# A GNN stack on one Trainium2 core: the minimum of the shared slots moved from VectorE to ScalarE in layer 0

## The reference

```
h    = max(layernorm(x), 0)
h_jk = relu(h_j @ W1a + (h_j - h_k) @ W1b + b1)      # for each edge j-k, 192 wide
hm_j = sum over k of mask[j,k] * h_jk
x    = x + hm @ W2 + degree * b2
```

## Time and profile before

| what | value |
|---|---|
| median of 3 runs | 1604.89 us (1604.22 to 1605.42) |
| the profiled execution | 1604.63 us |
| its span | 1602.8 us |
| TensorE busy | 1440.3 us (90%) |
| VectorE busy | 1273.2 us (79%) |
| ScalarE busy | 939.7 us (59%) |
| GpSimd busy | 493.8 us (31%) |
| mean granted TensorE clock | 0.971 |

### The profile page before, as it was taken

One profiled execution on the slowest core, in us unless ns is written; L12 is line 12 of the kernel. 1 busy time (PEld: TensorE's weight loads), 2 busy tenths in 40 slices (PEclk: granted clock), 3 DMA queues, 4 the chain that ended last, 5 costly groups with the idle time before them and its releaser, 6 DMA issues. The chain is left out here.

```text
span 1602.8 us, 42482 instructions
## 1 busy us (share of the span) xinstructions
PE 1440.3 (90%) x11815; PEld 1117.8 (70%) x11816; DVE 1273.2 (79%) x3215; ACT 939.7 (59%) x2169; POOL 493.8 (31%) x610
## 2 busy tenths in 40 slices
PE   0799999999999999999999999999799997973298
PEld 0577777777777777777777777777688887930298
DVE  6699999998999999999999999988344445878755
ACT  0756665666656566665666556653355554826675
POOL 1233333333333333333333333333111111047400
PEclk9999999999999999999999999999799999987599
DMA  6000000000000000000000000000000000000022
GB/s 139 14 8 9 14 7 7 7 7 13 7 7 7 7 13 7 7 7 7 13 7 7 7 7 7 6 1 1 1 0 0 0 0 1 0 0 1 3 49 53
DMA packets 40749, 18.09 MB, mean 11 GB/s; under 512 B 19396, under 2 KB 40710, under 8 KB 40710
## 3 DMA queue, kind: packets, MB, share of 16 engines
q1 hardware_dynamic: 40178, 17.39, 4.4%
q10 hardware_dynamic: 532, 0.21, 0.1%
HBM read 13.40 MB, written 4.19 MB: 11 GB/s over the span
## 5 line engine op out<-in xcount | busy, mean ns | idle before, releaser
L785 DVE SCALAR_TENSOR_TENSOR acc<-slot_banks,acc 128x768 f32<-128x768 f32 x512 | 488.1, 953 | 44.8 <-PE slot_banks L551 34.5
L849 POOL TENSOR_TENSOR acc<-acc 128x384 f32<-128x384 f32 x128 | 128.0, 1000 | 679.2 <-DVE onediff L779 675.4
L551 PE MATMUL slot_banks<-ac_hi,work 128*128 128x192 f16 x1408 | 263.9, 246 | 0.0
L551 PE MATMUL slot_banks<-ac_lo,work 128*128 128x192 f16 x1408 | 263.8, 246 | 0.0
L697 ACT ACTIVATE hmTa<-bank,unscale 128x128 f32<-128x128 f32 x128 | 47.0, 367 | 360.9 <-PE bank L527 360.9
L551 PE MATMUL slot_banks<-ac_hi,onediff 128*128 128x192 f16 x1024 | 186.0, 247 | 18.8 <-DVE acc L785 12.7
L551 PE MATMUL slot_banks<-ac_lo,onediff 128*128 128x192 f16 x1024 | 184.8, 246 | 0.0
L544 PE MATMUL slot_banks<-ac_hi,ident 128*128 128x384 f16 x512 | 168.0, 328 | 10.1 <-issue 9.5
L544 PE MATMUL slot_banks<-ac_lo,ident 128*128 128x384 f16 x512 | 167.0, 327 | 0.0
L551 PEld LDWEIGHTS slot_banks<-ac_hi,work 128*128 (+1 forms) x1408 | 137.9, 98 | 16.7 <-issue 0.2
L551 PEld LDWEIGHTS slot_banks<-ac_lo,work 128*128 (+1 forms) x1408 | 137.9, 98 | 16.7 <-issue 0.2
(11 more groups left out here) (251 smaller groups left out, 3283.9 us busy)
## 6 DMA issues: line engine op xcount, KB each, us to landing
adj_in<-in_adj_dram SPq DMA_DIRECT2D x32, 256.0 KB, 2.8
out_dram<-acc SPq DMA_DIRECT2D x32, 128.0 KB, 2.0
l1w<-in_L_gnn_W_dram SPq DMA_DIRECT2D x2, 64.0 KB
l1b<-in_L_gnn_b_dram SPq DMA_DIRECT2D x2, 64.0 KB
x_all<-in_x_dram SPq DMA_DIRECT2D x4, 0.2 KB, 12.0
nm_in<-in_nodemask_dram ACTq DMA_DIRECT2D x1, 64.0 KB
w1a<-in_L_gnn_W_dram ACTq DMA_DIRECT2D x1, 48.0 KB
w1b<-in_L_gnn_W_dram ACTq DMA_DIRECT2D x1, 48.0 KB
```

Of the source, the lines that this page charges most:

```text
L551: last = nc.tensor.matmul(unit(pair, t, 1), hot(t), part[:, q, H:2 * H].unsqueeze(1), start=False, stop=(e == 1 and (t % SB == SB - 1 or t ...
L785: nc.vector.scalar_tensor_tensor(out=sums, in0=unit((q + k) % 2, 0, SU), scalar=0.0, in1=sums, op0=ALU.min, op1=ALU.add).then_inc(s_free[k ...
L849: nc.gpsimd.tensor_tensor(acc[:, q, 0:2 * H], acc[:, q, 0:2 * H], acc[:, q, 2 * H:4 * H], ALU.add)
```

## The change

ScalarE takes the minimum of the shared slots, as Relu of the negative: `act_shared`. Relu(-v) is -min(v, 0), so the host matrix is copied with the scale -1, and the product of the two has the same value as before. `act_shared` for graph b - 1 stands at the head of ScalarE's step b, where VectorE had taken the minimum at the end of its step b - 1. The three slot rank copies leave `act_host_ranks` and become `act_host_slots`; they run in the following step 0, behind the copies of the product. `pool_sum` knew from VectorE's count of `s_free2` that VectorE's sums of the graph were made; for the last graph it now waits for `s_free[1]` too.

```
--- before.py
+++ after.py
@@ -417,7 +417,7 @@
         s_done = [sem(f"own_half{k}_gathered") for k in range(2)]
         s_free = [sem(f"own_half{k}_summed") for k in range(2)]
         s_done2 = sem("shared_slots_gathered")
-        s_free2 = sem("shared_slots_cut")
+        s_free2 = sem("shared_slots_summed")
         s_half = sem("neighbour_sums_paired")
         s_hm = sem("neighbour_sum_ready")
         s_T = sem("sum_transposed")
@@ -661,7 +661,10 @@
         def act_host_ranks(act, g, p):
             act.wait_ge(s_hr, g + 1)
             nc.scalar.activation(ranks2, pA3[:, :], ACT.Copy)
-            nc.scalar.activation(hostT[:, p, :], pH[:, :], ACT.Copy).then_inc(s_hostT, 1)
+            nc.scalar.activation(hostT[:, p, :], pH[:, :], ACT.Copy, scale=-1.0).then_inc(s_hostT, 1)
+
+        def act_host_slots(act, g, p):
+
             act.wait_ge(s_hostT, g + 1)
             for t in range(SS):
                 last = nc.scalar.activation(rs2[:, p, :, t, :], ranks2.rearrange("p (q j) -> p q j", q=GS),
@@ -691,6 +694,14 @@
             nc.scalar.activation(acc[:, q, :].rearrange("p (t h) -> p t h", t=SU),
                                  ac32[:, q % 2, 0:H].unsqueeze(1).broadcast_to([N, SU, H]), ACT.Relu,
                                  scale=neg_pad[:, p, q:q + 1]).then_inc(s_acc0, 1)
+
+        def act_shared(act, b, q):
+
+            if not (known(b) and b < 2):
+                act.wait_ge(s_hm, b - 1)
+            act.wait_ge(s_done2, b + 1)
+            nc.scalar.activation(acc2[:, q % 2, :].rearrange("p (t h) -> p t h", t=SS), unit(q % 2, 0, SS),
+                                 ACT.Relu, scale=-1.0).then_inc(s_free2, 1)
 
         def act_sum(act, b, p, q):
             act.wait_ge(s_T, b + 1)
@@ -818,11 +829,6 @@
                 dve.wait_ge(s_n, g1 + 1)
                 dve.reg_load(count_reg, chunks[0:1, ds(b + 1, 1)])
             late()
-            if not (known(b) and b < 2):
-                dve.wait_ge(s_hm, b - 1)
-            dve.wait_ge(s_done2, b + 1)
-            nc.vector.tensor_scalar(acc2[:, q % 2, :].rearrange("p (t h) -> p t h", t=SS), unit(q % 2, 0, SS),
-                                    0.0, None, ALU.min).then_inc(s_free2, 1)
 
         def dve_update(dve, b):
             xb = x[:, ds(b * F, F)]
@@ -846,6 +852,9 @@
             if not (known(b) and b == B - 1):
                 pool.reg_add(first, total, 1)
                 pool.wait_ge(s_D, first)
+            else:
+                pool.reg_add(first, total, B)
+                pool.wait_ge(s_free[1], first)
             nc.gpsimd.tensor_tensor(acc[:, q, 0:2 * H], acc[:, q, 0:2 * H], acc[:, q, 2 * H:4 * H], ALU.add)
             shared = acc2[:, q % 2, :]
             nc.gpsimd.tensor_tensor(shared[:, 0:H], shared[:, 0:H], shared[:, H:2 * H], ALU.add).then_inc(s_half, 1)
@@ -932,8 +941,11 @@
                 act_pads(act, 0, 0, 0, 0)
                 act_rank_nodes(act, 0)
                 act_host_ranks(act, 0, 0)
+                act_host_slots(act, 0, 0)
 
                 def step(b, g, u, q, nxt, p, use):
+                    if not (known(b) and b == 0):
+                        act_shared(act, b - 1, (q + 3) % GS)
                     if nxt is not None:
                         if q == 1:
                             act_rank(act, nxt, p)
@@ -943,6 +955,8 @@
                             act_rank_nodes(act, nxt)
                     if not (known(b) and b + 2 >= B):
                         act_ac(act, b + 2, (q + 2) % GS)
+                    if q == 0 and not (known(g) and g == 0):
+                        act_host_slots(act, g, u)
                     if not (known(b) and b + 1 >= B):
                         act_pads(act, b + 1, *group_of(b, g, u, q, -1))
                     if nxt is not None:
@@ -958,6 +972,7 @@
                         act_host_ranks(act, nxt, p)
 
                 all_iterations(act, step)
+                act_shared(act, B - 1, 3)
                 act_sum(act, B - 1, 1, 3)
 
             @block.vector
```

More of the change, by code:

```diff
@@ L820, in dve_slots @@
             late()
[L821 to L825, removed]
         def dve_update(dve, b):
```

## The result

The changed kernel takes 1609.62 us (median of 20 runs), the kernel before 1604.75 us (20 runs): ratio 1.0030, 95% interval 1.0023 to 1.0037. It is slower, as forecast, but by 4.9 us and not by 17.4; 1609.6 lies under the range. The profiled execution of the changed kernel has a span of 1608.5 us, 5.7 us over the one before.

A forecast was written before the change was run, and what follows sets the result against it. TensorE was 97% busy, with steps 2 and 3 starting on ScalarE's copy of the sum. A 1.28 us slip less 0.72 us gives 0.56 us a group; 31 groups add 17.4 us to 1604.6: 1622.0 us, range 1611 to 1633.

The forecast's parts named there:

- the idle time at its head: ScalarE's step 1: the minimum waits for the shared slots' last gather, rank copies queued behind it; 1.10 us of waiting.
- the price of the minimum: ScalarE's new instruction: 0.64 us long, delaying the next by 0.54 us, with bounds of 0.41 and 0.86 us.
- the slip of L698: ScalarE's second copy of the transposed sum in step 1 ends 1.28 us later, after 0.36 us are absorbed.
- the fixed 1.31 us: TensorE, steps 2 and 3: the graph's first half starts this long behind the end of ScalarE's copy of the sum.
- the 0.72 us that come back: TensorE's step 2: all that VectorE costs in a group, 0.72 us, goes by TensorE's own lateness.
- the + 0.56 us a group: Net loss per group of four graphs: 1.28 us of slip less 0.72 us, in 31 groups.
- steps 3, 0 and 1 keep their lengths: After step 2's transposes come 0.56 us later, everything following shifts equally and the other steps stay as long.
- priced at nothing: Edits given no cost: the minimum in steps 2, 3 and 0, the moved slot copies, the sign.
- (a): Rival: VectorE's relief in step 2 arrives without ScalarE's delay; 0.65 us a group, 20 us faster, 1584.5 us; 6%.
- (c): Rival: the minimum costs as much as the pads, 0.86 us to the next; 27 us lost, 1632 us; 12%.
- (d): Rival: minimum at its 0.41 us lower bound, 1618 us; with less than the whole 1.31 us paid, 1611; no separate chance.
- if one of the steps 2, 3 and 0 grew by itself: Sign in the changed profile that would show the forecast wrong; these steps were expected to have room for the edits.

The follow-up runs named there:

- run 9: The changed kernel with TensorE's load of the chunk count moved ahead of the product in every step: 1603.31 us, ratio 0.9987 to the kernel before.
- run 2: The changed kernel with only the step-0 graph's minimum on ScalarE, VectorE keeping the other three: 1619.08 us, ratio 1.0087 to the kernel before.
- run 3: The changed kernel with VectorE keeping the step-2 graph's minimum, ahead of step 3's difference: 1617.10 us, ratio 1.0075 to the kernel before.
- run 8: The changed kernel with a spare 256-element GpSimd addition ahead of the low part in step 3: 1617.60 us, ratio 1.0070 to the kernel before.
- run 4: The changed kernel with only the step-2 graph's minimum on ScalarE, VectorE keeping the others: 1601.18 us, ratio 0.9972 to the kernel before.
- run 11: The kernel before with only the three slot rank copies moved from the end of step 3 to step 0: 1604.78 us, ratio 0.9998.
- Run 1: The changed kernel with VectorE keeping the step-0 graph's minimum, so none heads ScalarE's step 1: 1591.81 us, ratio 0.9917 to the kernel before.
- run 6: The changed kernel with the minimum in step 1 behind the first three of eight rank copies: 1587.06 us, ratio 0.9890 to the kernel before.
- run 5: The changed kernel with ScalarE's copies of the sum moved ahead of `h` in step 1: 1603.97 us, ratio 0.9991 to the kernel before.

## Why the prediction was wrong

**Right, and shown.** The order of ScalarE's queue and the idle time at its head (1.26 us); the price of the minimum (0.66 us for 0.64, 0.55 to the next for 0.54); the slip of L698 (1.30 for 1.28); its way through the fixed 1.31 us, which run 9 shows to be the load of the chunk count (0.86 us without it). Right too were the 0.72 us that come back, by TensorE's lateness and not by VectorE's relief (run 2), and so the + 0.56 us a group (0.57).

**The step that failed** is "The transposes of step 2 ... come 0.56 us later, and steps 3, 0 and 1 keep their lengths". They don't. I had weighed VectorE's relief in step 2 alone and found it worth nothing there. The minimum is also gone in front of step 3's difference, and this was priced at nothing without asking what the earlier difference sets off. GpSimd waits for it to sum up the graph. Before, then in the change:

```profile
653.86 1.00 POOL L849 TENSOR_TENSOR acc<-acc 128x384 f32<-128x384 f32 x1 [4.52 <-DVE onediff L779]
```

```profile
659.50 0.99 POOL L858 TENSOR_TENSOR acc<-acc 128x384 f32<-128x384 f32 x1 [3.98 <-DVE onediff L790]
```

It starts 0.80 us behind step 3's first half (659.50 against 658.70) where it was 1.57 us (653.86 against 652.29). So its low part is over when VectorE makes the host rows, and these take 0.73 us for 1.23. The shared one-hot, again before and in the change:

```profile
658.73 0.31 DVE L773 TENSOR_SCALAR work<-work,slot_key 128x384 f16<-128x384 f16 x1
```

```profile
664.64 0.31 DVE L784 TENSOR_SCALAR work<-work,slot_key 128x384 f16<-128x384 f16 x1
```

It is ready 6.25 us behind step 3's first half, for 6.75, so 0.5 us earlier, and TensorE, which waits for it before it can pass the loop's back edge, finds its way over in time. Run 3 shows that this minimum decides, run 8 that it does so through GpSimd. It is worth 0.4 us in every second group. The loop's exit, some 2.5 us once, was priced at nothing too. Why TensorE needs about 2.1 us from the shared one-hot to the first half when the back edge lies between (661.11 - 659.04) is not shown; that it is the fetch of instructions is an argument only.

The Trainium skill (SBUF — State Buffer, Summary: rules for kernel authors) says that where VectorE is in a mode with two ports and GpSimd works at the same time, the second to issue blocks until the first is through. The rows agree: 0.5 us more for host rows that began 0.23 us behind a 0.92 us GpSimd instruction. In which mode VectorE runs them, no view here shows. The prediction never looked at these rows: it took the lengths of the steps as given, and the 0.5 us are in them. The groups' means show the same, 370 ns for one of the four before and 251 ns after.

**In numbers, for the two profiles.** 30 x 0.57 = 17.1 us of slip; 14 x 0.41 = 5.7 us less in the first groups of the loop's passes; 2.4 us less in the last group, which the loop's exit begins (steps 120 to 123 together 35.63 us before and 33.24 in the change, the slip included); 0.4 us less ahead of step 0; 2.7 us less behind layer 0, where the code is the same and kernels differ by up to 5.7 us. Together + 5.9 us, and the spans differ by 5.7. The 2.7 us are no effect of the change that a run shows: part of the distance between the forecast and the result may be chance. In the medians, too, all timed kernels but those of runs 4 and 11 lie 3 to 8 us under what 31 times their group would give (the change: 31 x 0.37 = 11.6 for 4.9 measured). In the change the last group explains about 3 of these; the rest stays open.

**The rivals.** (a), the faster one, priced VectorE's relief in step 2 at 0.65 us. Run 1 took ScalarE's delay away and found 0.1 us: the minimum had covered 0.42 us of issue behind the counts. Its total, 20 us, came to 13 us, and by another way. The rule beside it (the Trainium skill, Perfetto Trace Analysis, Optimizing Scalar/DVE Operations: offloading from a saturated DVE to Scalar may make sense), taken as a forecast, would have had the change faster; the traces do not bear that out for the change (ratio 1.003) and do for the same move three copies later in the queue (0.989, run 6). (c) and (d) were ranges of a price that was right; the doubt should have gone to the engines that I had not followed. That 1609.6 comes close to the 1611 of (d) is luck: the minimum cost 0.55 us and not 0.41, and the 1.31 us did not shrink. Of the signs named, the idle time, the 1.31 us, the waits and the minimum's length came as said; the group grew by 0.37 us and not by 0.56, and "if one of the steps 2, 3 and 0 grew by itself" was the right alarm with the wrong sign.

## What to carry to other kernels

Whether it pays to move an instruction from a full engine to a half-empty one depends on where it stands in that engine's queue. Here an instruction that waits for TensorE, put ahead of work that was ready, cost its wait (1.26 us) on top of its length (0.55 us), and three copies later in the queue turned 0.3% slower into 1.1% faster. When work leaves an engine, follow every signal that now comes earlier to the engines that start by it, GpSimd included, and look at what they ran beside before. And a long instruction between short ones may cover issue time of its engine, so its removal frees less than its duration: here 0.17 us of 0.67.

## What the runs showed of the hardware that was not expected

Four 16-bit instructions of VectorE took 0.73 us alone and 1.16 to 1.23 us beside a GpSimd instruction of 0.92 us; a 384-element one-hot took 0.81 us for 0.31 beside one (run 5). TensorE's first matmul behind a register load from SBUF started 1.31 us after the signal that both the load and a product had waited for, and 0.86 us after it when the load had been made before (run 9). Within 10 us of the first product behind the loop's exit VectorE stood idle once for 1.3 to 2.9 us, in every kernel. The wait view put this down to issue, and in the kernel before, in both its executions, to an engine that it did not wait for; where it came in the first half of step 120, that step was 2.3 to 2.7 us longer.
